# A corner of the transposed adjacency kept on chip, and late groups turned together with their source terms

## What is computed

```
A    = adj + I;  d = rsqrt(A.sum(axis=1));  An = d[:,None] * A * d[None,:]
h    = relu(An @ (x @ W1) + b1)
x    = layernorm(x + An @ (h @ W2) + b2)
x_norm = layernorm(x) * g1 + b1';   mask = (adj > 0) | I
for each head i:
    hi    = x_norm @ ff0[i].T
    e     = leaky_relu((hi @ a_src)[:,None] + (hi @ a_dst)[None,:]), -9e15 outside mask
    att   = layernorm(softmax(e, axis=1) @ hi + x) * g2 + b2'
    h_next += elu(att @ ff1[i].T) / 2
return layernorm(x + h_next)
```

## Time and profile before

| | us |
|---|---|
| median of three runs | 1020.89 |
| lowest and highest | 1017.95, 1023.19 |
| the profiled execution | 1018.46 |
| its span | 1015.4 |

### The profile page before, as it was taken

One profiled execution on the slowest core, in us unless ns is written; L12 is line 12 of the kernel. 1 busy time (PEld: TensorE's weight loads), 2 busy tenths in 40 slices (PEclk: granted clock), 3 DMA queues, 4 the chain that ended last, 5 costly groups with the idle time before them and its releaser, 6 DMA issues. The chain is left out here.

```text
span 1015.4 us, 9241 instructions
## 1 busy us (share of the span) xinstructions
PE 964.3 (95%) x2492; PEld 453.9 (45%) x2492; DVE 725.1 (71%) x1313; ACT 492.1 (48%) x756; POOL 187.1 (18%) x193
## 2 busy tenths in 40 slices
PE   5988989999999999999999999999999999999993
PEld 4333334444644444444555454444444444444541
DVE  1777766766565443426888777888779999888977
ACT  5343333221200000000088768778676888978774
POOL 1212223233059000004710001000000001010013
PEclk8999999999999999999999999999999999999997
DMA  9999999999579999993232232223212233313311
GB/s 380 419 420 419 418 417 417 415 417 399 243 288 381 379 395 377 387 392 149 87 102 80 65 94 72 94 62 104 68 57 93 84 104 94 104 63 94 94 52 42
DMA packets 69297, 223.88 MB, mean 220 GB/s; under 512 B 5318, under 2 KB 44806, under 8 KB 56710
## 3 DMA queue, kind: packets, MB, share of 16 engines
q1 hardware_dynamic: 65280, 209.67, 54.7%
q10 hardware_dynamic: 3974, 13.73, 3.4%
HBM read 203.43 MB, written 19.96 MB: 220 GB/s over the span
## 5 line engine op out<-in xcount | busy, mean ns | idle before, releaser
L1460 PE MATMUL ps<-T,Yw 128*128 128x512 f32 x1024 | 444.6, 593 | 1.0 <-DVE T L1107 0.6
L1460 PE MATMUL ps<-colbuf,stat 128*128 128x512 f32 x832 | 367.9, 602 | 23.3 <-DVE stat L899 23.3
L1133 DVE SCALAR_TENSOR_TENSOR T<-T,mring 128x2048 f32<-128x2048 f32 x125 | 286.0, 2289 | 63.2 <-ACT T L663 62.6
L663 ACT ACTIVATE T<-Rrow,small,ratio 128x1024 f32<-128x1024 f32 x250 | 294.8, 1231 | 61.5 <-PE ps L1460 61.3
L1460 PEld LDWEIGHTS ps<-T,Yw 128*128 128x128 f32 x1024 | 193.8, 190 | 237.9 <-issue 229.6
L1460 PEld LDWEIGHTS ps<-colbuf,stat 128*128 128x128 f32 x832 | 158.3, 192 | 228.9 <-issue 205.4
L582 ACT ACTIVATE W<-W 128x896 f32<-128x896 f32 (+15 forms) x57 | 67.9, 1191 | 136.1 <-DMA W<-in_adj 135.7
L961 DVE TENSOR_SCALAR mtile<-colbuf 128x4096 uint8<-128x4096 f32 x28 | 65.9, 2355 | 36.9 <-DMA mask<-mtile 36.2
L600 ACT ACTIVATE stat<-xw_g 128x128 f32 x20 | 6.2, 309 | 158.8 <-PE ps L1460 145.8
L524 POOL TENSOR_SCALAR rs<-sumsq 128x4 f32<-128x4 f32 x14 | 15.1, 1078 | 322.6 <-ACT squares L710 322.6
L471 POOL PARTITION_ALL_REDUCE colrow<-W x31 | 33.3, 1075 | 184.8 <-DVE W L860 164.4
(11 more groups left out here) (198 smaller groups left out, 682.5 us busy)
## 6 DMA issues: line engine op xcount, KB each, us to landing
colbuf<-in_adjT SPq DMA_DIRECT2D x64, 1024.0 KB, 16.7
colbuf<-in_adjT SPq DMA_DIRECT2D x24, 2048.0 KB, 10.5
mring<-mask SPq DMA_DIRECT2D x128, 256.0 KB, 2.7
mask<-mtile ACTq DMA_DIRECT2D x26, 512.0 KB, 10.1
W<-in_adjT SPq DMA_DIRECT2D x4, 2048.0 KB, 11.0
Rrow<-s_src SPq DMA_DIRECT2D x9, 512.0 KB, 4.1
W<-in_adj SPq DMA_DIRECT2D x4, 960.0 KB, 15.4
W<-in_adj SPq DMA_DIRECT2D x4, 896.0 KB, 16.0
```

Of the source, the lines that this page charges most:

```text
L663: last = act.activation(T[:, c % TS, j, :], Rrow[:, g % 2, :], ACT.Relu, scale=ratio[:, c * JB + j:c * JB + j + 1], bias=small[:, 8:9])
L1133: v.scalar_tensor_tensor(out=tile, in0=tile, scalar=1.0, in1=mring[:, c % TS, :, :].rearrange("p b n -> p (b n)"), op0=ALU.add, op1=ALU.mu ...
L1460: return pe.matmul(*args, skip_group_check=True, **kw)
```

## The change

1. `corner`, 128 x 16 x 512 in float32 (16 row blocks of the transpose, its first four blocks of columns), is loaded right after x, in two transfers of eight row blocks. Rows 0 to 3 are summed from column 2048 on alone, the first sixteen column blocks are loaded from column 512 on, and TensorE takes group 0 of these blocks from `corner`. VectorE reduces the corner over its row blocks, the first half at once, the second for each of the blocks 0 to 3. Buffers are moved so that it fits (`early_rows`, `colrow`, `colown`, `gain_mix`).
2. Groups 2 to 7 (k >= WHOLE) are turned by products with `turner`, the identity with the four source columns beside it, 132 columns in place of 128; two blocks go to the group's bank and two to the bank of group k - 2, so each turn waits for the normalisation of that group. ScalarE copies the source terms out to `raw_st`. Groups 0 and 1 keep transposes, with their `sources` behind the late sums of group 2.
3. ScalarE normalises, with scale and bias, where VectorE did; GpSimd computes the bias `shift`, and one factor `comb` for the product of `rstd` and `r2` straight from the variance. For the last group `comb` comes before `rstd`. `r2` is made later, as `comb / rstd`.
4. Z uses three banks. The last group is normalised behind `read_z(2)`. TensorE has `multiply_z` 0 to 4 ahead of the product that spreads the maximum, then 5 to 7 ahead of the first chunk.

```diff
+        corner = sb("corner", [P, CR, CB * P], F32, held)
...
-            lo, mid = b * P, (b + (B - b) // 2) * P
+            from_block = CR if b < CB else b
+            lo, mid = from_block * P, (from_block + (B - from_block) // 2) * P
...
+            if b < CR:
+                return slice(CB * P, N // 2), slice(N // 2, N)
...
-        Z_FIRST, Z_BANKS, Z_WAITING = 4, 4, 8
+        Z_FIRST, Z_BANKS, Z_WAITING = 4, 3, 8
+        TW = P + 2 * K
+        WHOLE = 2
...
+            for k in range(CP):
+                sp.dma_start(corner[:, cols(k, CR // CP), :], corner_cols[:, cols(k, CR // CP), 0:CB * P]).then_inc(corner_loaded[k], 16)
...
-            for k in range(NG):
+            for k in range(NG - 1):
                 scale_rows(k)
-                scale_again(k)
+                scale_both(k)
+            scale_both(NG - 1)
+            scale_rows(NG - 1)
...
+            def normalise(k):
+                act.wait_ge(scale_ready, k + 1)
+                for b in range(k * BPG, (k + 1) * BPG):
+                    last = act.activation(x1[:, b, :], turned(b), ACT.Identity, scale=rstd[:, b:b + 1], bias=shift[:, b:b + 1])
+                last.then_inc(x1_ready, 1)
...
-            for r in range(2, Z_FIRST):
+            read_z(2)
+            normalise(NG - 1)
+            for r in range(3, Z_FIRST):
                 read_z(r)
...
+            def over_corner(out, rows, columns, done):
+                v.tensor_reduce(out, corner[:, rows, columns].rearrange("p j n -> p n j"), AX_X, ALU.add).then_inc(done, 1)
+
+            def corner_sums(b):
+
+                own = cols(b)
+                over_corner(colacc[:, own], slice(CR // CP, CR), own, corner_summed)
+                v.wait_ge(corner_summed, b + 2)
+                v.tensor_tensor(colacc[:, own], colacc[:, own], corner_part[:, own], ALU.add).then_inc(colown_done, 1)
+
+            v.wait_ge(corner_loaded[0], 16)
+            over_corner(corner_part[:, :], slice(0, CR // CP), slice(0, CB * P), corner_summed)
+            v.wait_ge(xw_done, NG)
+            v.wait_ge(corner_loaded[1], 16)
+            corner_sums(0)
...
             def turn_sums(k):
+
                 pe.wait_ge(raw_ready, k + 1)
+                if k >= WHOLE:
+                    pe.wait_ge(x1_ready, k - 1)
+                    pe.wait_ge(raw_st_ready, 1)
                 for ib in range(BPG):
-                    last = pe.transpose(ps[:, k, cols(ib)], raw_sums[:, cols(k * BPG + ib)], ident[:, :])
+                    own = raw_sums[:, cols(k * BPG + ib)]
+                    if k < WHOLE:
+                        last = pe.transpose(ps[:, k, cols(ib)], own, ident[:, :])
+                    else:
+                        last = multiply(ps[:, k if ib < 2 else k - 2, cols(ib % 2, TW)], own, turner[:, :], start=True, stop=True)
                 last.then_inc(tr_done, 1)
...
+                if k == WHOLE:
+                    for own in range(WHOLE):
+                        sources(own)
-                if k == EARLY - 1:
+                if k == EARLY:
                     pe.wait_ge(early_ready, 1)
-                if k >= 3:
-                    sources(k - 3)
...
-            for r in range(4, Z_WAITING):
+            for r in range(5, Z_WAITING):
                 multiply_z(r)
```

More of the change, by code:

```diff
@@ L127, in build @@
         rstd = sb("rstd", [P, B], F32)
+        comb = sb("comb", [P, B], F32)
+        eps_both = sb("eps_both", [P, B], F32)
+        neg_mean = sb("neg_mean", [P, B], F32)
+        shift = sb("shift", [P, B], F32)
+        turner = sb("turner", [P, P + 2 * K], F32)
         r2 = sb("r2", [P, B], F32)
@@ L316, in more_passes, with turned @@
             return eng.value_load(npass[0:1, 0:1], min_val=0, max_val=MAX_PASSES)
+        def turned(b):
+            k, ib = b // BPG, b % BPG
+            if k < WHOLE:
+                return ps[:, k, cols(ib)]
+            return ps[:, k if ib < 2 else k - 2, ib % 2 * TW:ib % 2 * TW + P]
         def late(n):
@@ L869, in _ @@
-                v.wait_ge(colpart_step, 3 * b + 1)
+                    v.wait_ge(colacc_done, b - 1)
+                    v.tensor_tensor(colacc[:, own], colacc[:, own], colbuf[:, before, own], ALU.add).then_inc(colown_done, 1)
+                elif b + 1 < CB:
+                    corner_sums(b + 1)
+                v.wait_ge(colrow_ready, b + 1)
+                v.tensor_tensor(colown[:, :], colrow[:, b % 2, :], ident[:, :], ALU.mult).then_inc(colpart_step, 1)
+                v.wait_ge(colpart_step, 3 * b + 1)
@@ L1492, in aggregate_halves @@
             def aggregate_halves(u, turn, b):
+                if b < CR:
+                    multiply(ps[:, 0, :], stat[:, u, :], block_of(corner, turn * RING + u), start=False, stop=False)
                 for groups, landed in zip(near_groups(b), (near_loaded[u], col_loaded[u])):
@@ L1495, in aggregate_halves @@
                     for k in groups:
-                        last = multiply(ps[:, k, :], stat[:, u, :], colbuf[:, u, cols(k, GW)], start=False, stop=False)
+                        if k > 0 or b >= CR:
+                            last = multiply(ps[:, k, :], stat[:, u, :], colbuf[:, u, cols(k, GW)], start=False, stop=False)
                 last.then_inc(pe_block, 1)
@@ L1574, in sources @@
                     b = k * BPG + ib
-                    last = multiply(ps[:, 0, cols(b, 2 * K)], raw_sums[:, cols(b)], wag[:, :], start=True, stop=True)
+                    last = multiply(ps[:, 0, OWN_ST + b * 2 * K:OWN_ST + (b + 1) * 2 * K], raw_sums[:, cols(b)],
+                                    turner[:, P:TW], start=True, stop=True)
                 last.then_inc(st_done, 1)
@@ L1610, in _ @@
             last.then_inc(mix_turned, 1)
-            for k in range(NG - 3, NG):
-                sources(k)
             multiply_z(0)
```

188 lines of the change are left out of this document (105 added, 83 removed).

## The result

The changed kernel takes **1024.93 us** (median of 19 runs), the kernel before in the same measurement 1021.63: ratio 1.0036, 95% interval [1.0024, 1.0047], some 3.5 us slower. That is inside the 0.5% that the forecast took as "the same", though the interval lies clear of 1. The forecast was 1024.8. That the two agree to 0.1 us is luck, as the comparison of the two profiled executions shows: there it is 1024.93 us (span 1023.1) against 1018.46 (span 1015.4), 6.5 us instead of the 3.9 of the sum.

What follows compares the result with a forecast made beforehand. TensorE, 95% busy, was the bound, with DMA behind its early waits and VectorE close. Terms −7.2 + 9.0 + 2.1 = +3.9 us gave 1022.4 on the profiled execution, 1024.8 us for the median; its own range was 1021 to 1029.

Steps and rivals of the forecast that it cites:

- start, `stat` of block 0: First aggregation's start: corner loads and VectorE's reductions (4.4 and 1.2 us) put block 0's `stat` at 24.5, +2.6 us.
- `stat` of block 4: First aggregation, blocks 1 to 4: savings of 1.5, 0.6 and 0.5 us cancel the late start, sum 0.
- blocks 5 to 16: First aggregation: VectorE's waits for row sums and a column block go, gaining 7.2 us; then VectorE is the bound.
- first turn to the spread maximum: Late groups up to the product spreading the reference: it moves from 514.55 to 516.2, +1.65 us.
- rest of the Z stall: Eighth Z product waits for ScalarE before the first chunk: +9.0 us by the third chunk's end, 1.65 us of it counted earlier.
- half clock behind it: After the idle stretch before the first chunk, TensorE runs at the 1.2 GHz level: +2.1 us, ends 0 to 2.4.
- rival A: First aggregation: VectorE reads the corner slowly, first reduction over 5 us; total +12 us, 1033; chance 0.13.
- Rival C: First stage yields little, loads bunch up and DMA stays the bound: gain 3 us, total +8, 1029; chance 0.19.
- TensorE's gaps before block 16: Sign in the profile after: these gaps shrink by about 7 us, or the prediction is wrong.
- The gain passes through unchanged: From block 17 to 467 us: same matmuls, no TensorE gap, loads and masks follow, so the 7.2 us gain stays whole.
- Rival B: Z stall short or absent, as ScalarE reaches `read_z(4)` long before TensorE needs it: −5.6 us, 1015.3; chance 0.10.
- The offset: From profiled execution to median: the one before lies 2.4 us below its median of 1020.89, so 1022.4 became 1024.8.

Runs made afterwards that it cites:

- after_filled: The changed kernel with 36 products of zeros in TensorE's idle time before the stalling Z product; 1022.24 us, ratio 1.0007.
- seven_unit_stride: z_seven with the corner's reductions, same size, run over neighbouring elements, which are the wrong ones to sum; 1011.85 us (one run).
- corner_alone: The kernel before with only the corner added (loads, sums, stationary blocks), late groups and Z banks as before; 1013.21 us, ratio 0.9927.
- z_nine_before: The kernel before with nine Z products ahead of the first chunk instead of eight; 1029.33 us, ratio 1.0079.
- late_alone: The changed kernel without the corner: new late groups, three Z banks, eight products ahead of the first chunk; 1030.34 us, ratio 1.0087.
- corner_again: Same kernel as corner_alone, run in the second set; 1015.31 us, ratio 0.994.
- corner_third: Same kernel as corner_alone, run on one chip with seven_again in more rounds; 1013.6 us, ratio 0.9927.
- seven_again: Same kernel as z_seven, run on one chip with corner_third in more rounds; 1015.36 us, ratio 0.9946.
- z_seven: The changed kernel with seven Z products ahead of the first chunk instead of eight; 1014.84 us, ratio 0.9936.
- corner_adds: corner_alone with the corner's sums made by additions of whole rows in place of reductions; 1012.88 us, ratio 0.9916.
- corner_mixed: corner_alone with the corner's first half summed by additions of whole rows, the second by reductions; 1013.01 us, ratio 0.9918.
- seven_adds: z_seven with the corner's sums made by additions of whole rows, all four blocks' ahead of block 0; 1015.01 us, ratio 0.993.

## Why the prediction came out, point by point

| step of the sum (us, profiled executions) | forecast | measured |
|---|---|---|
| start, `stat` of block 0 | +2.6 | +6.1 |
| `stat` of block 4 against before | 0 | +3.2 |
| blocks 5 to 16 | −7.2 | −8.9 |
| first stage, at block 16 | −7.2 | −5.7 |
| first stage, at the late groups | −7.2 | −6.5 |
| from there to the first turn | 0 | +1.8, not the change's |
| first turn to the spread maximum | +1.65 | +1.6 |
| rest of the Z stall, to the end of the third chunk | +7.35 | +7.5 |
| half clock behind it | +2.1 | +2.9 |
| behind the third chunk | 0 | +0.4 |

The last three rows come from three traces. From the spread maximum to the end of the third chunk it is 15.45 us in the kernel before, 22.95 in after_filled, which has the stall at full clock, and 25.89 in the changed kernel. From there to TensorE's last product it is 469.2 us before and 469.0 after, and from that product to the end of the span 16.2 and 16.8; in every other run this last part takes 16.1 to 16.4, so its +0.5 is a matter of this one execution. The measured steps from the late groups on (−6.5, 1.8, 1.6, 7.5, 2.9, 0.4) add up to the span's 7.7, and since 1.8 us lie around the span of the changed kernel against 3.1 before, the 6.5 of the two execution times.

**The start** failed in three places. The corner's second half can be taken up at 19.6, not 18.6, but that is hidden under the step that cost most: the first reduction takes 7.15 us instead of 4.4 and ends at 21.1. Then the small one 1.9 instead of 1.2. And block 1's reduction, 2.2 us with its add, stands in front of block 0's diagonal, whose all-reduce takes only 1.1; I had given block 0 the usual wait of 1.2. Together 28.00 instead of 24.5. The mechanism of rival A is real, then (its point of decision was 5 us, and seven_unit_stride shows the step in memory as the cause). The rule of the Trainium skill cited with it ("Advanced Engine Details and Errata", section "Memory Cachelines") agrees with that run; the size, which it leaves open, is here 1.75 ns an element against 1.08. But its price was wrong by far: 1.3 us at the late groups, not 8. I had added each late microsecond to the bare chain without asking what the later blocks give back.

**Blocks 5 to 16** gave 8.9 where 7.2 were booked. The mechanism was right: in that stretch VectorE's waits for row sums and for a column block (6.7 and 1.1 us) are gone, and nothing came in their place. The size was off on the overlap: operations that follow each other without a wait start about 0.1 us before the end of the one ahead (the addition of 2.95 us at 104.20 is followed by the degree step at 107.07), so each wait that goes frees about 0.1 more than it shows. I had subtracted 0.05 each. Between block 16 and the late groups another 0.8 us came in: TensorE's run in the earlier trace rows ends at 193.9 us, where the kernel before waits once more for `stat` (0.37 us before 194.31), while the changed kernel has no gap behind 146.45.

```profile
104.20 2.95 DVE L911 TENSOR_TENSOR W<-W,colbuf 128x2688 f32<-128x2688 f32 x1
107.07 0.21 DVE L952 SCALAR_TENSOR_TENSOR small<-rowpart,colpart 128x1 f32<-128x1 f32 x1
```

Two errors of opposite sign, +3.2 and −1.7, and the 0.8 behind block 16 thus lie under a first stage that came out 0.7 us short. Rival C (a gain of only 3) is refuted by it and by corner_alone.

One sign that the forecast named did not come: TensorE's gaps before block 16 were to shrink by about 7 us. A line of each kernel up to `stat` of block 16, then one behind block 4 (columns as in the earlier trace rows):

```profile
0.00:158.80 158.80, 129.83 (x328) 59.14 (x328) 101.50 (x270) 63.09 (x95) 35.43 (x44) 0.96 1.00 412
56.80:158.80 102.00, 88.72 (x192) 36.75 (x192) 73.13 (x194) 37.08 (x60) 25.57 (x24) 0.97 1.02 418
```

```profile
0.00:153.10 153.10, 126.62 (x327) 58.48 (x328) 114.25 (x278) 56.89 (x95) 38.49 (x46) 0.96 1.01 408
60.00:153.10 93.10, 85.07 (x192) 35.48 (x192) 72.05 (x194) 36.19 (x60) 25.56 (x24) 1.00 1.02 418
```

TensorE's idle time fell from 29.0 to 26.5 us, by 2.5, since the late start added 6 us of it. The other 3.2 of the 5.7 lie in its busy time: behind block 4 it has the same 192 records in both, at a mean clock of 0.97 before and of 1.00 after. So the count of gaps was the wrong place to read the gain; the start of `stat` is the right one.

**"The gain passes through unchanged"** fails in the profiled run: of 6.5 us 4.7 reach the first turn, above all because a late column block lands after it is wanted (the 1.42 us above). It is not the change, though. From the late groups to the first turn the kernel before took 11.41 us in its profiled run, but z_nine_before, which is the same up to there, 12.27, and late_alone, which has no corner, 13.28; corner_alone, corner_again and corner_third, three runs of one kernel, 11.65, 12.94 and 12.57; seven_again 13.65 and after_filled 11.32, against 13.20 in the changed kernel, of which both are copies up to there. The profiled run of before was one where the block came in time. What decides when it comes was not tried.

**The late groups** came out as worked out: products of 132 columns, the wait for group 0 (0.80 instead of 1.1), the combined scale and the last normalisation on the way to the reference make +1.6. TensorE in the changed kernel, the wait for group 0 and the last turn:

```profile
470.58 1.95 PE L1535 MATMUL ps<-turner,W 128*128 128x4 f32 x16 [0.80 <-ACT W L677]
...
503.78 1.17 PE L1535 MATMUL ps<-turner,W 128*128 128x132 f32 x8 [0.79 <-DVE W L1086]
```

**The Z stall** is the step that set the sign, as said. It was read off the order of ScalarE's instructions and the banks. The length of the stall came out as forecast (7.5 us for 7.35). The clock was sized too small because the low level outlasted the 4.8 us of work taken for it; from the stalled product to the one behind the third chunk it is 14.21 us (523.09 to 537.30) against 11.27 in after_filled (523.03 to 534.30), 2.9 us for the 2.1 of the sum. To the end of the span z_seven, without stall and fall, gains 10.1 us on the changed kernel behind the spread maximum (501.6 against 511.7). Rival B (no stall) is refuted.

**The offset, and the luck.** The sum on the profiled executions was 3.9 us and came out at 6.5, of which 1.8 is the late column block. The 2.4 us from the profiled run of before to its median were added on the footing that a profiled run stands to its kernel's median as another does; after, it stands at the median. The profiled run of before lies 3.2 us below its kernel's median of 19. Part of that can be named: it has no late column block and no fall of the clock in the late groups, where other runs have one or the other; whether that is all of it is not shown. So the 1024.8 rests on a sum 2.6 us too small and an offset 2.4 us too large for this pair of executions, and that the two cancel is luck. Between the two medians of 19 the difference is 3.3 us (3.7 by the ratio), so there the sum of 3.9 is near; but its terms were off by up to 1.8 us in both directions.

## What to carry to other kernels

A product that is issued ahead of a phase on the promise of a free bank must be counted again when the number of banks changes: banks and products ahead go in pairs, and here one digit was worth 10 us, more than all that a saved transfer had brought. An idle stretch of the bound engine is paid twice where its clock falls; if the stretch can't be removed, products of zeros in it bring back the second part (2.9 us here). And a saving in front of a gapless stretch is read at the first record behind that stretch, not at the start: a start 1 us later or 3 us earlier came out within 0.2 us of each other.

## What the runs showed of the hardware

- VectorE's reduction of f32 in SBUF at a 2 KB step takes 1.75 ns an element per partition (7.15 us for 4096), the same reduction of neighbouring elements 1.08 (4.42).
- TensorE's granted clock fell to its 1.2 GHz level without any recorded idle time near it, among products four columns wide: for 6.8 us each in corner_again, corner_adds and corner_mixed, and not at all in four other runs of the same products (before, z_nine_before, corner_alone, corner_third). In seven_adds and after_filled it fell for 3.4 us near 471 us, behind sixteen such products with 0.8 us of idle time ahead of them; the changed kernel, z_seven and seven_again have the same products and the same 0.8 us, and no fall.
- The falls cost 3.1 and 1.7 us of the stretch up to the spread maximum, so together with the column block's landing (0 to 1.9 us) they are large enough for much of the 3 to 5 us by which runs of one kernel differ. The mean clock of whole executions leans the same way: of the kernel before in the three sets, only the three executions with 0.989 or 0.990 took less than 1019.5 us. Whether it is the whole of that, and what makes the clock fall there, stays open.
